# Attention's output kept in one plane and split in the first FFN, with new orders in the blocks and at the end of attention

## The reference, cut to what matters

```python
q = rms_norm((x @ wq).reshape(B, L, 16, 128), q_norm_w)
k = rms_norm((x @ wk).reshape(B, L, 4, 128), k_norm_w)
...
q = q * cos + rotate_half(q) * sin
k = k * cos + rotate_half(k) * sin
k_full = jnp.concatenate([k_ctx, k], axis=1)
...
scores = jnp.einsum('blhd,bmhd->bhlm', q, k_full) * scale + mask
probs = jax.nn.softmax(scores, axis=-1)
out = jnp.einsum('bhlm,bmhd->blhd', probs, v_full)
return out.reshape(B, L, 2048) @ wo
...
x = x + attention(layernorm(x), ctx)
x = x + ffn(layernorm(x), w1, w2)
```

## Time and profile before

| | us |
|---|---|
| median of 3 runs | 1550.41 (1549.67 to 1550.69) |
| the profiled execution, its own time | 1556.07 |
| span of its trace | 1554.7 |
| TensorE busy | 1447.8, 93% |
| VectorE busy | 1136.8, 73% |
| ScalarE busy | 982.5, 63% |
| GpSimd busy | 950.8, 61% |

### The profile page before, as it was taken

The page is one execution under the profiler, slowest core; times in us unless marked ns, Lnnn a source line. Parts: engine busy times, 40 slices in busy tenths (PEclk is TensorE's granted clock), DMA queues, the critical chain, the costliest instruction groups (busy, mean ns, idle before and its releaser), DMA issues. The chain is left out here.

```text
span 1554.7 us, 24273 instructions
## 1 busy us (share of the span) xinstructions
PE 1447.8 (93%) x7729; PEld 1095.2 (70%) x7772; DVE 1136.8 (73%) x2460; ACT 982.5 (63%) x2246; POOL 950.8 (61%) x770
## 2 busy tenths in 40 slices
...
DMA packets 84318, 164.77 MB, mean 106 GB/s; under 512 B 39392, under 2 KB 39648, under 8 KB 82784
## 3 DMA queue, kind: packets, MB, share of 16 engines
...
HBM read 112.86 MB, written 41.94 MB: 100 GB/s over the span
## 5 line engine op out<-in xcount | busy, mean ns | idle before, releaser
L393 PE MATMUL bank<-wq,xT 128*128 128x512 f32 x768 | 208.8, 414 | 5.3 <-ACT wq L533 4.3
L1334 PE MATMUL bank<-wq,ot 128*128 128x512 f32 x768 | 185.0, 399 | 15.1 <-POOL wq L1125 10.0
L423 PE MATMUL quad<-qT,kT 128*128 128x512 f32 x672 | 192.3, 418 | 5.3 <-issue 5.3
L862 DVE TENSOR_TENSOR PT<-P,PT 128x1024 fp32r<-128x1024 f32 (+1 forms) x128 | 151.8, 1186 | 44.8 <-ACT PT L643 43.5
L439 PE MATMUL bank<-PT,vv 128*128 128x512 f32 x672 | 175.6, 401 | 8.3 <-DVE OT L892 6.6
L393 PEld LDWEIGHTS bank<-wq,xT 128*128 128x128 f32 x768 | 146.1, 191 | 51.7 <-issue 20.2
L1334 PEld LDWEIGHTS bank<-wq,ot 128*128 128x128 f32 x768 | 146.2, 191 | 48.6 <-issue 10.4
L1632 POOL TENSOR_TENSOR cl<-cl,fixed 128x1 f32<-128x1 f32 x16 | 8.8, 551 | 273.7 <-DVE cl L1516 273.7
L439 PEld LDWEIGHTS bank<-PT,vv 128*128 128x128 f32 x672 | 123.0, 189 | 41.8 <-DVE PT L862 10.4
L423 PEld LDWEIGHTS quad<-qT,kT 128*128 128x128 f32 x672 | 119.9, 189 | 39.4 <-issue 20.8
L1070 POOL TENSOR_TENSOR small<-small,fixed 128x6 f32<-128x6 f32 (+1 forms) x66 | 115.5, 1750 | 32.8 <-DVE small L797 32.6
...
## 6 DMA issues: line engine op xcount, KB each, us to landing
ot_scratch<-OT SPq DMA_DIRECT2D x64, 512.0 KB, 2.7
ot<-ot_scratch SPq DMA_DIRECT2D x64, 512.0 KB, 5.5
wkv_f<-in_w SPq DMA_DIRECT2D x12, 512.0 KB, 6.3
wkc_f<-in_w SPq DMA_DIRECT2D x12, 512.0 KB, 7.0
wkv_f<-in_wg SPq DMA_DIRECT2D x11, 512.0 KB, 6.9
wkv_f<-in_wd SPq DMA_DIRECT2D x11, 512.0 KB, 6.9
wkv_f<-in_wu SPq DMA_DIRECT2D x10, 512.0 KB, 7.0
...
```

Source lines behind the costliest of these rows:

```text
L393: ins = pe.matmul(bQ[:], xT[p][:, k, qt * 128:qt * 128 + 128], wq[j][:, g, k, :], start=(part == 0 and k == 0), stop=(part == 2 and k == 3))
L423: ins = pe.matmul(quad[:, c, :], kT[x][:, bg % 2, c * 128:c * 128 + 128], qT[y][:], start=(n == 0), stop=(n == 2))
L862: dve.tensor_tensor(lo, P[:, c[0]:c[-1] + 1, :], hi.bitcast(F32), ALU.subtract).then_inc(f["pt_lo"], 1)
L1334: ins = pe.matmul(y_bank(n)[:], ot[:, c % 4, i, k * 128:k * 128 + 128].bitcast(F32R), wo[j][:, g, k, :], start=(g == 0 and k == 0 and q == ...
```

## The change

It does six things.

- O is stored in one plane (256 KB a block). VectorE writes it, SyncE stores it, and the split into high and low part is made after it is loaded in `ffn0`: for c from 8 on by GpSimd (`pool_ot`, two instructions), for c from 0 to 7 the high part by ScalarE (`act_ot`) and the low one by GpSimd. `pool_ot` stands in GpSimd's program right after `pool_rs(n)`, four at a time.
- The copy of the own keys moves from VectorE (`dve_k_n`) to ScalarE (`act_k_copy`).
- The third term of an odd block's sum moves from VectorE to GpSimd: `pool_t_pair` makes two additions there and now waits for the second exponential.
- Orders in the blocks change on all engines. In odd blocks both parts of the scores come together, and `pe_sum` after `pe_pv(i - 1, 0)`; in even ones the first third of the query product comes ahead of `pe_pv(i - 1, 0)`, except in the turn block, and the sum after the scores. `dve_p_lo(i - 1, 0)` of an odd block moves into the even block after it. Both outputs of a pair are made in the odd block.
- SyncE issues the loads of the last eight blocks one block earlier, and those for blocks 63 and 64 after that block's output is stored.
- The pieces of the next stage's weights come at other places: GpSimd's eight `pool_wo` in blocks 59 to 64 instead of 57 to 64, with four `pool_ot` in 62 to 64; ScalarE's at the ends of blocks.

The diff, cut:

```diff
@@ -265,6 +264,7 @@
...
                 ffn["sp_ot"](c)
+        if i == 63:
             sp_w2_sums(1)
@@ -295,15 +295,18 @@
...
             p = i - 1
-            sp_last(i)
+            if i + 1 <= 62:
+                sp_last(i + 1)
             if b + 1 < NB and r == 6:
...
                 sp_x(2 * b + 3)
-            sp.wait_ge(f["o_lo"], p + 1)
-            sp.dma_start(ot_dram[2 * (p // 8) + p % 2, p // 2 % 4], OT[:].bitcast(F32)).then_inc(f["ot0"], 16)
+            sp.wait_ge(f["o_n"], p + 1)
+            sp.dma_start(ot_dram[2 * (p // 8) + p % 2, p // 2 % 4], OT[:]).then_inc(f["ot0"], 16)
+            if i > 62:
+                sp_last(i)
@@ -463,14 +466,14 @@
...
         pe_s(i, 0)
+        pe_s(i, 1)
         if i == 63:
             ffn["pe_y"](0, 0)
+        pe_pv(i - 1, 0)
+        pe_q(i + 2, 0)
         pe_sum(i - 1)
-        pe_q(i + 2, 0)
-        pe_pv(i - 1, 0)
+        pe_k_turn(i + 2)
         pe_pv(i - 1, 1)
-        pe_k_turn(i + 2)
-        pe_s(i, 1)
         pe_q(i + 2, 1)
@@ -483,19 +486,23 @@
...
         pe_s(i, 0)
+        if not turn and i > 4:
+            pe_q(i + 2, 0)
         if i == 64:
...
             pe_x_turn(2 * (i // 8) + 3)
+        pe_s(i, 1)
+        if turn or i <= 4:
+            pe_q(i + 2, 0)
         pe_sum(i - 1)
-        pe_s(i, 1)
-        for part in range(3):
-            pe_q(i + 2, part)
+        pe_q(i + 2, 1)
+        pe_q(i + 2, 2)
         pe_k_turn(i + 2)
...
         pe_pv(i - 1, 1)
-        if i == 60:
+        if i == 62:
             pe_w1_sum()
@@ -547,6 +554,14 @@
...
+    def act_k_copy(u):
+
+        if u >= NU:
+            return
+        act.wait_ge(f["kv_mm"], u + 1)
+        after(act, f["kt_mm"], u)
+        act.copy(kn, kv4(u)[:, 0]).then_inc(f["k_n"], 1)
+
     def act_k_sq(u):
@@ -661,11 +670,12 @@
...
         if i > 56:
-            for p in {(57, 0): (0,), (58, 0): (1,), (59, 0): (2,), (60, 0): (3,), (61, 0): (4,), (62, 1): (5,),
-                      (63, 0): (6,), (63, 1): (7,)}.get((i, half), ()):
+            for p in {(58, 1): (0,), (59, 1): (1,), (60, 1): (2,), (61, 1): (3,), (62, 0): (4,), (62, 1): (5,),
+                      (63, 1): (6,), (64, 0): (7,)}.get((i, half), ()):
                 act_wo(p)
-            for q in {(61, 1): (0,), (61, 2): (1,), (62, 0): (2,), (62, 1): (3,), (63, 1): (4,), (64, 0): (5,),
-                      (64, 1): (6, 7)}.get((i, half), ()):
+            for c in {(62, 1): (0,), (63, 1): (1,), (64, 0): (2,), (64, 1): (3,)}.get((i, half), ()):
+                ffn["act_ot"](c)
+            for q in {(63, 1): (0, 1), (64, 0): (2, 3), (64, 1): (4, 5, 6, 7)}.get((i, half), ()):
                 act_w2_abs(q)
@@ -673,47 +683,42 @@
...
         act_q_sq(i + 1)
+        act_k_copy(i + 2)
         act_k_sq(i + 2)
         act_v_hi(i + 2)
-        act_last(i, 0)
         act_exp(i, 0)
-        act_o_hi(i - 2)
-        act_p_hi(i)
+        act_exp(i, 1)
         if i < 4:
...
         act_q_n(i + 1)
-        act_exp(i, 1)
+        act_p_hi(i)
+        act_p_hi(i, 1)
         act_last(i, 1)
-        act_last(i, 2)
...
         act_q_hi(i)
-        act_p_hi(i - 1, 1)
         if i <= 4:
...
             act_x_hi(2 * (i // 8) + 2)
-        act_o_hi(i - 2)
         act_exp(i, 0)
...
             act_x_hi(2 * (i // 8) + 3)
-        act_last(i, 0)
-        act_exp(i, 1)
         if i <= 4:
...
         act_q_n(i + 1)
+        act_exp(i, 1)
+        act_last(i, 0)
         act_k_hi(i + 2)
-        act_p_hi(i)
         if i % 8 == 4 and i + 4 < NBLK:
...
             act_c_hi(2 * (i // 8) + 3)
-        if i == NBLK:
-            act_o_hi(i - 1)
+        act_p_hi(i)
         act_last(i, 1)
@@ -800,14 +806,10 @@
...
         after(dve, f["kt_mm"], u)
-        if unit(u)[1]:
-            dve.wait_ge(f["kv_mm"], u + 1)
-            dve.tensor_copy(kn, kv4(u)[:, 0]).then_inc(f["k_n"], 1)
-        else:
-            dve.wait_ge(f["norms"], k_normed(u))
-            dve.wait_ge(f["v_hi"], u + 1)
-            dve.tensor_tensor(kn, kv4(u)[:, 0], k_norm(u).unsqueeze(2).broadcast_to((128, 2, 128)),
-                              ALU.mult).then_inc(f["k_n"], 1)
+        dve.wait_ge(f["norms"], k_normed(u))
+        dve.wait_ge(f["v_hi"], u + 1)
+        dve.tensor_tensor(kn, kv4(u)[:, 0], k_norm(u).unsqueeze(2).broadcast_to((128, 2, 128)),
+                          ALU.mult).then_inc(f["k_n"], 1)
@@ -866,20 +868,17 @@
...
         dve.wait_ge(f["p_own"], 2 * i + 1)
-        if i % 2:
-            v.did(dve.tensor_tensor(t, t, P[:, 2, :], ALU.add))
-            v.settle()
         dve.tensor_tensor(t, t, P[:, 2 + i % 2, :], ALU.add).then_inc(f["t_add"], 1)
...
         dve.wait_ge(f["sum_mm"], i + 1)
-        dve.transpose(sT[:], bT[:]).then_inc(f["s_ri"], 1)
+        dve.transpose(ri[:], bT[:]).then_inc(f["s_ri"], 1)
...
         dve.wait_ge(f["s_ri"], i + 1)
-        v.did(dve.reciprocal(rsum, sT[:].rearrange("p (c n) -> p c n", n=32)[:, :, 0]))
+        v.did(dve.reciprocal(rsum, ri[:].rearrange("p (c n) -> p c n", n=32)[:, :, 0]))
         v.settle()
@@ -889,7 +888,7 @@
...
         v.settle()
-        dve.tensor_tensor(OT[:, 1, :].bitcast(F32), bO[:], ri[:], ALU.mult).then_inc(f["o_split"], 1)
+        dve.tensor_tensor(OT[:], bO[:], ri[:], ALU.mult).then_inc(f["o_n"], 1)
@@ -928,13 +927,11 @@
...
             dve_w(2 * i + 6)
+        dve_o(i - 2)
         dve_t_sum(i - 1)
-        dve_k_n(i + 2)
-        if i > 1:
-            dve_p_lo(i - 1, 0)
-        dve_o(i - 2)
+        dve_p_lo(i - 1, 0)
+        dve_p_lo(i - 1, 1)
         dve_ve(i)
-        dve_p_lo(i - 1, 1)
         dve_v_lo(i + 2)
@@ -943,9 +940,9 @@
...
         dve_s_turn(i - 1)
-        dve_p_lo(i, 0)
         dve_k_lo(i + 2)
         dve_ri(i - 1)
+        dve_o(i - 1)
         if prep:
@@ -956,15 +953,14 @@
...
             dve_ln_b(2 * (i // 8) + 3)
-        dve_o(i - 2)
         dve_t_sum(i - 1)
+        dve_p_lo(i - 1, 0)
         if turn:
...
         dve_p_lo(i - 1, 1)
-        dve_s_turn(i - 1)
         if turn:
@@ -976,11 +972,11 @@
...
         dve_last(i, 0)
-        if i == NBLK:
-            mem["dve_ternary"](0, 3)
+        dve_s_turn(i - 1)
         dve_ri(i - 1)
...
             dve_o(i - 1)
+            mem["dve_ternary"](0, 3)
         dve_k_lo(i + 2)
@@ -1108,16 +1102,14 @@
...
             return
-        pool.wait_ge(f["s_exp"], 2 * i + 1)
+        pool.wait_ge(f["s_exp"], 2 * i + 1 + i % 2)
         after(pool, f["sum_mm"], i)
-        pool.tensor_tensor(tt[:], P[:, 0, :], P[:, 1, :], ALU.add).then_inc(f["t_add"], 1)
-
-    def pool_o_lo(i):
-        if i < 0:
-            return
-        pool.wait_ge(f["o_split"], 2 * i + 2)
-        pool.tensor_tensor(OT[:, 1, :], OT[:, 1, :].bitcast(F32), OT[:, 0, :].bitcast(F32),
-                           ALU.subtract).then_inc(f["o_lo"], 1)
+        pair = pool.tensor_tensor(tt[:], P[:, 0, :], P[:, 1, :], ALU.add)
+        if i % 2:
+            g_.did(pair)
+            g_.settle()
+            pair = pool.tensor_tensor(tt[:], tt[:], P[:, 2, :], ALU.add)
+        pair.then_inc(f["t_add"], 1)
@@ -1132,10 +1124,8 @@
...
         pool_t_pair(i)
-        pool_o_lo(i - 2)
         pool_mask(i)
-        if i >= 57:
-            pool_wo(i - 57)
+        pool_last(i)
@@ -1143,15 +1133,18 @@
...
         pool_mask(i)
-        pool_o_lo(i - 2)
         pool_p_hi(i)
...
             pool_c_lo(2 * (i // 8) + 3)
-        if i == NBLK:
-            pool_o_lo(i - 1)
-        if i >= 58:
-            pool_wo(i - 57)
+        pool_last(i)
+
+    def pool_last(i):
+
+        for p in {59: (0,), 60: (1,), 61: (2,), 62: (3, 4), 63: (5,), 64: (6, 7)}.get(i, ()):
+            pool_wo(p)
+        for c in {62: (0,), 63: (1,), 64: (2, 3)}.get(i, ()):
+            ffn["pool_ot"](c)
@@ -1232,7 +1225,7 @@
...
                 sp.wait_ge(f["ot0"], 16 * NBLK)
-            sp.dma_start(ot[:, c % 4, :, :], ot_dram[c // 4, c % 4]).then_inc(f[f"g_ot{c % 4}"], 16)
+            sp.dma_start(ot[:, c % 4, 1, :], ot_dram[c // 4, c % 4]).then_inc(f[f"g_ot{c % 4}"], 16)
@@ -1322,13 +1315,13 @@
...
         c = 4 * n + g
-        pe.wait_ge(f[f"g_ot{c % 4}"], 16 * (c // 4 + 1))
+        pe.wait_ge(f["ot_lo"], c + 1)
         if n == 0:
...
             if n == 1:
-                pe.wait_ge(f["o_lo"], NBLK)
+                pe.wait_ge(f["o_n"], NBLK)
         for k in range(4):
@@ -1461,10 +1454,15 @@
...
         act.wait_ge(f["w_gamma"], 2)
+        act_ot(4)
+        act_ot(5)
         for q in (5, 6, 7):
...
             act_xq(n)
+            if n == 0:
+                act_ot(6)
+                act_ot(7)
             if n == 0:
@@ -1625,6 +1623,21 @@
...
+    def act_ot(c):
+        act.wait_ge(f[f"g_ot{c % 4}"], 16 * (c // 4 + 1))
+        act.copy(ot[:, c % 4, 0, :].bitcast(F32R), ot[:, c % 4, 1, :]).then_inc(f["ot_hi"], 1)
+
+    def pool_ot(c):
+
+        if c >= 4 * NT:
+            return
+        hi, lo = (ot[:, c % 4, j, :].bitcast(F32R) for j in range(2))
+        if c >= 8:
```

(16 more changed lines are left out.)

31 lines of the change are left out of this document (12 added, 19 removed).

## The result

The changed kernel takes 1555.61 us (median of 8 runs, 1552.45 to 1558.59) where the kernel before takes 1550.95 in the same rounds (8 runs, 1549.67 to 1552.45). The ratio is 1.0032, 95% interval 1.0019 to 1.0045. The forecast was 1545.8, faster by 4.6; it is slower by 4.7, inside the range.

A forecast was written before the change was run, and what follows sets the result against it. TensorE, busy 93% of the span, was taken to bound the kernel, with losses in turn blocks and at attention's end. +3 - 14.4 + 2 + 3.7 + 2.6 - 1.5 = -4.6, from 1550.4 to 1545.8 us; range 1534 to 1560.

The forecast's parts named there:

- C: Block 62 to the FFN's first tile: GpSimd's order decides, +2 us, bounds -4 and +5.
- A: Blocks up to 56: ordinary pairs pay nothing, about +0.4 in each of 7 turns, +3 us, bounds -7 and +8.
- B: Blocks 57 to 61: earlier loads remove ScalarE's 12.7 us of waits, -14.4 us, bounds -17.4 and -9.
- D: Start of the FFN: ScalarE waits for the load of `ot(7)`, its queued work is delayed, +3.7 us, bounds 0 and +6.
- E: First FFN's tiles: GpSimd's splits may delay `xh`, 0.2 a tile, +2.6 us, less 1.5 for lighter loads.
- the sum's ring: Block 63: `pe_y(0,0)` waits for GpSimd and holds `pe_sum(62)` behind it, for which `pool_t_pair(63)` waits, until S+24.
- My note on `pe_y(1, 0)`: First FFN's tile 1: TensorE was to wait about 5 us at `pe_y(1, 0)`.
- the TENSOR_SCALAR that I had called harmless: GpSimd's 1.50 us instruction: a VectorE addition with two SBUF inputs had run undelayed, 0.68 us, within it.
- Rival 1: Gain of blocks 57 to 61 reaches the end, as later slack is larger: 1538 or 1535 us, chance 0.18.
- Rival 2: All given back, from block 62 on or in turn blocks; wait moves to GpSimd's queue: 1550 to 1553, chance 0.20.
- Rival 3: Ordinary pairs stall at `pe_pv(i - 1, 0)` in even blocks, 0.6 us in each of 28: 1563 us, chance 0.20.
- the prediction's own signs of failure: Ordinary pair over 24.2, tiles over 18.7, or TensorE not waiting for GpSimd's work in the last eight blocks.

The follow-up runs named there:

- e4: The kernel before, with only SyncE's loads of the last blocks issued one block earlier: 1535.60 us, ratio 0.9904 to the kernel before.
- e1: The changed kernel, with block 62's sum (and the first output product) ahead of `pe_y(0, 0)` on TensorE in block 63: 1550.95 us, ratio 1.0001 to the kernel before.
- e10: Three-order kernel (sum first, splits after `xh`, low part first), with `pe_y(0, 1)` and `pe_y(0, 2)` moved behind the last output product: 1529.16 us, ratio 0.9850 to before.
- e3: The changed kernel, with `dve_p_lo(i - 1, 0)` ahead of the sum's last addition on VectorE in even blocks: 1541.73 us, ratio 0.9946 to the kernel before.

## Why the prediction was wrong

The sum came out with the wrong sign: -4.6 forecast, +4.7 measured. One step did it, C, forecast at +2 and measured at +11.9; an error of 3.2 in A went the other way. The rows at both ends of each step are in the windows and timelines above; time is counted on TensorE.

| step | forecast | in the traces | how it comes out |
|---|---|---|---|
| A, start to block 57 | +3 | -0.2 | 751.04 to 750.81 |
| B, blocks 57 to 61 | -14.4 | -14.7 | 80.41 to 65.71 |
| C, block 62 to `pe_x_turn(0)` | +2 | +11.9 | 59.15 to 71.09 |
| D, to `pe_x_turn(1)` | +3.7 | +2.8 | 17.27 to 20.07 |
| E, the rest | +1.1 | +2.1 | 646.8 to 648.9 |
| sum | -4.6 | +1.9 | 1554.7 to 1556.6 |

**A was half right, by two errors that cancel.** An ordinary pair is 24.01, a batch 99.97, within the 99 to 100 forecast. TensorE's waits from 40 to 760 in the changed kernel (the counterpart of the earlier trace rows, over a longer window):

```profile
PE bank L442 <- DVE PT L864: 15.9, 16, 1.7
PE bank L378 <- POOL kk L1076: 3.3, 7, 0.5
```

The turn block's wait is 1.7 where I had 1.1, and the ordinary pair's 0.08 I had at nothing; over the six batches from block 9 to block 56 the price is 6.1 us (595.86 to 601.95), where +0.4 in each of seven turns made 3. Against it stands what I had not looked for: all up to block 9 is 6.3 us shorter (it starts at 148.86 instead of 155.18, and at 148.79 when the kernel was run again). The windows up to block 9, of before and then of after, show how:

```profile
0.00:155.18 155.18, 134.14 (x677) 107.31 (x678) 114.40 (x193) 98.10 (x265) 110.57 (x87) 0.95 0.26 96
```

```profile
0.00:148.86 148.86, 129.94 (x677) 103.41 (x678) 115.33 (x184) 96.18 (x263) 106.38 (x84) 0.99 0.25 92
```

The matmuls are the same 677. They take 4.2 us less at a granted clock of 0.99 instead of 0.95, and 2.1 us of idle time are gone. Which of the moved parts frees the first blocks was not tried.

**B was right in size, and for the larger part in reason.** ScalarE has no wait for `wq_in` there. e4, with the loads alone, gains 11.1 of the 14.7 us (69.3 us for the five blocks); the other 3.6 belong to the rest of the change, and which part of it gives them was not tried.

**C is the step that failed, mis-sized.** The mechanism was as put. GpSimd's queue sets the products' starts, and the sum's ring sets GpSimd's. I had the starts at S+17.9, S+32, S+40 and the end at S+46. They came at S+20.4, S+36.7, S+46.5 and S+55.3. Each link is 1.7 to 2.9 us longer, and together they make the last output product 9.3 late, which is the whole error of C (9.9) but for 0.6. Two sizes were wrong. GpSimd's additions, low and high parts had been given their undelayed times and its pieces their mean, and only a little was added in B for what two engines do to each other, though the earlier trace rows had already shown 2.30 for 0.68: a low part took 2.24 and 1.71 instead of 1.3, a piece 3.34, a high part 2.46 instead of 1.5, about 4 us in the chain. And the last link, on TensorE alone, was given 6 us and took 8.85. The rest is mostly the pair sum of block 62, at S+8.6 instead of S+6.7, behind TensorE's scores, its wait of 1.08 for a low part and the lower clock. The windows from block 62 to `pe_x_turn(0)`, of before and of after, say what that left out:

```profile
831.45:890.60 59.15, 38.35 (x138) 28.25 (x138) 41.12 (x51) 27.07 (x44) 29.73 (x18) 0.86 0.51 191
```

```profile
816.52:887.61 71.09, 45.48 (x140) 33.46 (x141) 50.13 (x58) 31.20 (x49) 41.49 (x23) 0.76 0.35 118
```

The work is the same but for two matmuls. TensorE is idle 25.6 us where it was idle 20.8, and busy 45.5 where it was busy 38.4: of the 11.9 us, 4.8 are longer waits and 7.1 the longer matmuls, at a granted clock of 0.76 instead of 0.86. The two clocks alone would give 5.0 of these (38.35 x 0.86 / 0.76 = 43.4, an estimate); what the other 2 are is open. My lower bound of -4 assumed all terms a fifth shorter; the upper one, +5, had neither effect in it. e1 takes the sum out of the ring for 7.8 us, e10 takes two products out of attention's queue for 5 to 8. No run parts what GpSimd and VectorE do to each other from what the clock does.

**D was right within a microsecond, for a partly wrong reason.** ScalarE waits 1.20 for `ot(7)`, not 4. It goes from `act_xq(0)` to `act_relu` in 9.24 us instead of 7.35, with two copies, 1.2, and that wait in it; the rest of D is `xn` and `xh` of tile 1 (0.83 and 1.10), longer by 0.9 together than in a steady tile of before. My note on `pe_y(1, 0)`, about 5 us, was 4.40.

**E: 0.42 a steady tile instead of 0.2**, 4.6 us over twelve tiles. Two early tiles differ more. From the transposes of tile 1 to those of tile 2 it takes 2.2 us longer (20.41 instead of 18.21), from tile 3 to tile 4 5.1 less (18.83 instead of 23.88; before, TensorE stood there for a DMA of `hh`, 1.52, and for ScalarE, 2.27, which had waited some 8 for weights). So some 3 us came back where I had 1.5; that the lighter loads of O did it is not shown. The delay came where it was looked for, but `xn` is delayed too, by the TENSOR_SCALAR that I had called harmless. The Trainium skill, "SBUF — State Buffer", section "SBUF: two separate sides", says that whichever of the two starts first keeps the shared ports for its whole instruction, if VectorE's operation has two inputs in SBUF (and GpSimd's reads SBUF) or runs in a mode that takes two ports. Taking `xn` and `xh` to run in such a mode, which no run here shows: by that rule `xh`, started 0.46 into a subtraction of 1.29, would wait some 0.8; it lost 0.63, so here the trace is near it. `xn` started at 962.25, 0.06 into a TENSOR_SCALAR of 1.50, and lost 0.28 instead of 1.4, so for that form it is not borne out. GpSimd in the same tile:

```profile
962.19 1.50 POOL L1637 TENSOR_SCALAR ot<-ot 128x512 fp32r<-128x512 f32 x1
963.77 1.29 POOL L1639 TENSOR_TENSOR ot<-ot 128x512 fp32r<-128x512 f32 x1
```

**The rivals.** Rival 1 is excluded. Rival 2 is what happened, with the last blocks the place, at somewhat more than its price. That price was added up too low: with C, D and E at their own upper bounds (+5, +6, +7.8 less 1.5) the terms give 1556, not 1553. The upper bound of B was a slip too: 63.0 and six times 1.5 are 72.0, not 71.4. Rival 3's place is right and its size is not: an ordinary pair is 0.08 longer, not 0.6, and the wait is in the turn block. Its other half, that a delayed VectorE holds `pe_pv(i - 1, 0)`, is what e3 removed.

None of the prediction's own signs of failure came: an ordinary pair is under 24.2, a tile under 18.7, and GpSimd is what TensorE waits for. No sign gave the last blocks a length, so none could catch the step that failed. And that the time still lies between 1534 and 1560 is in part luck: had block 9 not come 6.3 us earlier, it would be near 1562 (an estimate from these two numbers).
